# Attention with hardware loops over batches and head groups instead of unrolled code

## The reference

```python
q = (x @ Wq).reshape(b, s, 32, 32);  k, v = split(x @ Wkv)
scores = einsum('bqhd,bkd->bhqk', q, k) * 32**-0.5 + slope[h] * (kpos - qpos)   # causal
out = einsum('bhqk,bkd->bqhd', softmax(scores), v).reshape(b, s, h) @ Wo
x = layernorm(x + out)
rank = (8, 16, 32, 64)[argmax(x @ gate_w.T + gate_b)]
x = layernorm(x + x @ W.T + bias + (x @ A[:rank].T) @ B[:, :rank].T)
```

## Time and profile before

| | |
|---|---|
| time, median of 3 runs | 4088.18 us (4086.85 to 4093.12) |
| the profiled execution | 4086.85 us, span of its instructions 4085.0 us |
| PE busy | 3766.8 us, 92% of the span |
| DVE, ACT, POOL busy | 2474.2, 1925.0 and 1360.6 us |
| attention | up to about 3187 us of the span |
| feed-forward tiles | from about 3250 us to the end, 25.9 us each |

### The profile page before, as it was taken

One profiled execution on the slowest core, in us unless ns is written; L12 is line 12 of the kernel. 1 busy time (PEld: TensorE's weight loads), 2 busy tenths in 40 slices (PEclk: granted clock), 3 DMA queues, 4 the chain that ended last, 5 costly groups with the idle time before them and its releaser, 6 DMA issues. The chain is left out here.

```text
span 4085.0 us, 56649 instructions
## 1 busy us (share of the span) xinstructions
PE 3766.8 (92%) x22065; PEld 2354.1 (58%) x22065; DVE 2474.2 (61%) x4462; ACT 1925.0 (47%) x3253; POOL 1360.6 (33%) x420
## 2 busy tenths in 40 slices
PE   5989989999999997888999999999998599999998
PEld 3555555555454543555555554544443488888887
DVE  4557767776767672555776777676764344444444
ACT  2435655665666664344665666566666211111110
POOL 1113434444445453112433444455555100000000
PEclk8879999999999998888999999999999799999999
DMA  2111110000000001211111000000000412111111
GB/s 71 40 53 32 32 42 22 22 22 22 14 19 14 19 6 34 60 37 45 32 30 45 19 22 22 14 22 13 20 14 3 145 62 62 61 57 57 57 60 52
DMA packets 158918, 150.73 MB, mean 37 GB/s; under 512 B 8388, under 2 KB 141508, under 8 KB 156584
## 3 DMA queue, kind: packets, MB, share of 16 engines
q1 hardware_dynamic: 158696, 147.70, 12.4%
HBM read 96.75 MB, written 33.62 MB: 32 GB/s over the span
## 5 line engine op out<-in xcount | busy, mean ns | idle before, releaser
L494 ACT ACTIVATE prob<-ps_s,alibi 128x512 f32<-128x512 f32 (+3 forms) x2560 | 1521.6, 623 | 1110.5 <-PE ps_s L756 545.6
L574 DVE TENSOR_REDUCE mxp<-ps_a 128x1 f32<-128x512 f32 (+3 forms) x2560 | 1457.8, 605 | 800.7 <-PE ps_a L695 418.4
L437 POOL TENSOR_TENSOR prob<-prob 128x2048 f32<-128x2048 f32 (+1 forms) x240 | 1044.4, 4351 | 1126.5 <-ACT prob L494 1126.5
L756 PE MATMUL ps_s<-qst,kexp 97*128 97x512 f32 (+3 forms) x2560 | 1092.3, 437 | 74.5 <-ACT prob L494 55.1
L692 PE MATMUL ps_a<-kmax,qst 97*128 97x512 f32 (+3 forms) x2560 | 956.1, 399 | 34.3 <-DVE mxp L574 17.3
L756 PEld LDWEIGHTS ps_s<-qst,kexp 97*128 97x128 f32 x2560 | 492.3, 194 | 727.6 <-ACT prob L494 425.1
L779 PE MATMUL ps_o<-prob,val 128*32 128x512 f32 (+3 forms) x5120 | 612.2, 551 | 7.7 <-ACT prob L494 7.7
L692 PEld LDWEIGHTS ps_a<-kmax,qst 97*128 97x128 f32 x2560 | 504.3, 198 | 116.7 <-DVE mxp L574 59.5
L779 PE MATMUL ps_sum<-prob,ones 128*32 128x512 f32 (+3 forms) x3200 | 361.4, 525 | 0.0
L965 POOL TENSOR_TENSOR hb_sb<-h_sb,bias_b 128x1024 f32<-128x1024 f32 x32 | 76.8, 2401 | 791.9 <-DVE z_sb L1109 732.2
L592 DVE RECIPROCAL r_sb<-s_sb 128x128 f32<-128x128 f32 x256 | 233.4, 928 | 113.8 <-ACT s_sb L500 113.1
(11 more groups left out here) (148 smaller groups left out, 3709.3 us busy)
## 6 DMA issues: line engine op xcount, KB each, us to landing
wq_raw<-in_L_attn_Wq SPq DMA_DIRECT2D x65, 512.0 KB, 4.0
xs<-in_L_attn_hidden_states SPq DMA_DIRECT2D x9, 2048.0 KB, 8.7
qst<-qst SPq DMA_DIRECT2D x64, 256.0 KB
att_scratch<-at_sb SPq DMA_DIRECT2D x64, 256.0 KB, 2.4
at_raw<-att_scratch SPq DMA_DIRECT2D x32, 512.0 KB, 5.3
x_sb<-in_L_attn_hidden_states SPq DMA_DIRECT2D x32, 512.0 KB, 4.3
out<-z_sb SPq DMA_DIRECT2D x32, 512.0 KB, 3.2
z_sb<-in_L_attn_Wo SPq DMA_DIRECT2D x4, 512.0 KB, 5.1
```

The source lines that it names most:

```text
L437: nc.gpsimd.tensor_tensor(even[:, :, c1:], even[:, :, c1:], odd[:, :, c1:], ALU.add).then_inc(pair_done, 1)
L494: nc.scalar.activation(prob[slot][:, h, c0:], ps_s[bank][:, c0:], ACT.Exp, bias=alibi_of(u, h, k - QT * s)).then_inc(e_done, 1)
L574: nc.vector.tensor_reduce(mxp[:, h * QT + t, c:c + 1], ps_a[bank][:, 0:cols], AX.X, ALU.max).then_inc(a_done, 1)
L756: last = nc.tensor.matmul(ps_s[bank][:, c0:], kexp[0:KR, k * P:(k + 1) * P], qst[buf][0:KR, h, c0:], start=True, stop=not diagonal)
```

## The change

The loop over b becomes a hardware loop of 2 iterations. For s = 1, 2 and 3 the units 0 to 5 become a hardware loop of 2 iterations with 3 units in its body; units 6 and 7, and all units of s = 0, stay written out inside the loop over b. Buffers are picked by a number modulo 3, so three units in the body leave the buffers right. The order of the engine instructions stays the same. `counts` now moves its three totals into registers at the start of each unit.

```diff
-            for b in range(B):
+            with eng.Fori(0, B) as b:
                 prologue(b)
                 for s in range(NSEG):
                     more = s + 1 < NSEG
-                    for u in range(HG - 2):
-                        unit_step(b, s, u, u, plan_step(s, True, s, True, False, s > 0 or u > 0))
+                    if s == 0:
+                        for u in range(HG - 2):
+                            unit_step(b, s, u, u, plan_step(s, True, s, True, False, u > 0))
+                    else:
+                        with eng.Fori(0, 2) as i:
+                            for j in range(3):
+                                unit_step(b, s, i * 3 + j, j, plan_step(s, True, s, True, False, True))
                     unit_step(b, s, HG - 2, HG - 2, plan_step(s, True, s, more, more, True))
                     unit_step(b, s, HG - 1, HG - 1, plan_step(s, more, s + 1, more, False, True))
                 epilogue(b)
...
-        def counts(b, s, u):
-            return unit_no(b, s, u), START + b * TILES_B + tiles_before(s, u), START + b * STEPS_B + steps_before(s, u)
+        taken = []
+
+        def counts(eng, b, s, u):
+            taken.append(eng)
+            values = (unit_no(b, s, u), START + b * TILES_B + tiles_before(s, u),
+                      START + b * STEPS_B + steps_before(s, u))
+            regs = [eng.alloc_register(f"{name}_{len(taken)}") for name in ("unit", "tiles", "steps")]
+            for reg, value in zip(regs, values):
+                eng.reg_mov(reg, value)
+            return tuple(eng.snap(reg, min_val=low) for reg, low in zip(regs, (0, START, START)))
```

More of the change, by code:

```diff
@@ L424, in step @@
             def step(b, s, u, const, plan):
-                g, tiles, steps = counts(b, s, u)
+                g, tiles, steps = counts(pool, b, s, u)
                 for what, arg in plan:
@@ L476, in step @@
             def step(b, s, u, const, plan):
-                g, tiles, steps = counts(b, s, u)
+                g, tiles, steps = counts(act, b, s, u)
                 for what, arg in plan:
@@ L605, in step @@
             def step(b, s, u, const, plan):
-                g, tiles, steps = counts(b, s, u)
+                g, tiles, steps = counts(dve, b, s, u)
                 i = 0
@@ L719, in step @@
             def step(b, s, u, const, plan):
-                g, tiles, steps = counts(b, s, u)
+                g, tiles, steps = counts(pe, b, s, u)
                 buf = parity(s, const)
```

## The result

The changed kernel takes 4186.7 us in the median of 4 runs (4184.06 to 4193.92), the kernel before 4087.5 beside it: 1.0243 times as long, with a 95% interval of 1.0225 to 1.0261. That is 99 us more. The forecast was 4151 us, within 4118 to 4195. Direction and main mechanism held; the sum of 64 us was too small by a third.

The account below looks back on a forecast made before the run. The prediction took PE as the bound, held up by the latency loop between its scores and ACT's exponentials. Terms of 50 + 4 + 10 = 64 us on the profiled 4086.85 us gave 4151 us, range 4118 to 4195.

Parts of the forecast that it names:

- What bounds the kernel: Attention's score-exponential loop: PE bounds the unit, but latency exceeds its work, 1.28 us against 0.94 for two slots.
- Exponentials in the looped units: ACT, looped units: two register operations behind the score wait add 0.18 us on 276 turns, 50 us (41 to 61).
- Exponentials elsewhere: ACT in s = 0 and units 6 and 7: the register operation runs before the wait, so nothing is added.
- PE's register operations: Ahead of nearly each score matmul on PE: cost nothing, since PE's sequencer runs ahead of its array.
- PE's lead is lost at each wait: Rival, PE's score matmuls: register operations show twice each turn, 61 us more, 4212 us; chance 0.09.
- DVE's shift, and SP: End of looped units: one operation behind DVE's `c_max` wait, 4 us; `c_ps` and SP operations 0, at most 4.
- Loop edges: Six inner edges and one over b: taken branches wait for code, 1.4 us each, 10 us (2 to 25).
- edges cost much more: Rival, loop edges: engines' code misses add up to 76 us in place of 10, 4217 us; chance 0.06.
- Which edges miss: ACT's loop edges: s = 2, 3 and the outer miss, s = 1 may not, making the term 9 us for 10.
- Faster: Rival, PE's score loads: idle time without releaser is code fetching, loops save 73 us, giving 4078 us; chance 0.04.
- the dearer rivals: PE's lead lost at each wait (4212 us, chance 0.09) and edges costing much more (4217 us, chance 0.06).

Follow-up runs that it names:

- the copied bias: Changed kernel, with POOL copying the next unit's 64 bias columns to a fixed buffer so that ACT's bias address is constant: 4131.6 us, ratio 1.0087.
- the pauses kernel: Kernel before the change, with PE waiting for a POOL memset ahead of six units of s = 3, no branch added: one run, 4116.6 us.

## Why the prediction was right, and where its sum was short

*What bounds the kernel.* Held. The loop of latencies between score and exponential passed on the added 0.19 us in full: the turn was forecast at 1.46 us and is 1.47.

*Exponentials in the looped units.* Forecast 50 us, and right in size and cause. Taking the operations out of the looped kernel gives back 50 us by the units (48 with the copied bias), and adding them without a loop costs 48. I had 4, 7.5 and 11.5 turns for the three s; the growth by 0.59, 1.36 and 2.33 us with ACT alone looped, at 0.19 each, is 3.1, 7.1 and 12.1. The errors nearly cancel, 22.3 for my 23. The duration, taken from DVE's row, was right for ACT.

*Exponentials elsewhere, and PE's register operations.* Forecast nothing, and nothing is seen: gap 0.04 us in units 6 and 7, PE's steady units unchanged with PE alone looped. The rival "PE's lead is lost at each wait" falls with that.

*DVE's shift, and SP.* Forecast 4 us, at most 4 more. The steady units keep 8 us when ACT's operations are out, and 10.6 with DVE, POOL and SP looped alone, of which 4 go when DVE is written out. So DVE's 4 us fit; the row of waits that I priced them from doesn't show them, since PE's wait for the shift is 63.9 us in the changed kernel, for 65.9 before. What POOL and SP add, 7 us when looped without the others, I had bounded at 4.

*Loop edges.* This is the mis-sized term: 10 us forecast, 30 measured at the six inner edges and some 3 at the outer one, beyond my upper end of 25. I took 1.4 us an edge from the smallest landing, "a little of it covered by PE's lead". With PE alone looped an edge that misses costs 6.4 us: a stall of about 3.4 and then 3.0 for the half clock behind it; in the changed kernel the six cost 2.5 to 6.4, 4.9 on average. The upper end of 3.6 us for the stall would have been near (PE's branches take 3.5 to 3.6); the clock was in no part of my sum. The gap on ACT, forecast at 1 to 2 us, is 2.5 to 3.1 from its branch to the next operation. I had rows for a stall and asked only how long PE stands still, not what it runs at afterwards. Nor does PE's lead cover anything at an inner edge, since its own branch stalls. The rival "edges cost much more" named the wrong mechanism: the misses of engines do not add up (27 and 27 us alone, 30 together).

*Which edges miss.* By the rule of the Trainium skill ("Runtime: NRT & Kernel Launch", "Instruction fetch mechanics") I let the edge of s = 1 pass on ACT, whose body of 450 instructions is shorter than the 512 named there. (The loop of s = 1 has an edge in each b, so that the term would have been 7 us and not 9.) It missed: unit 3 of s = 1 took 39.57 us at 0.96. At 269 instructions, with the copied bias, it did not. The same section has the code come in blocks of 256 instructions and the window hold two of them, so a body of 450 can reach into a third; I had compared only its length. That the place counts is seen on DVE in the feed-forward loop, whose body of 266 instructions the change doesn't touch: its next operation stands 0.33 to 0.37 us behind the branch in the kernel before, and 2.95 to 3.00 in the changed one (at no cost, as the tiles are still 25.89 us apart). On PE, counting a weight load and its matmul as two, the body of s = 1 has 1592 instructions and was at hand, and that of s = 2 has 2183 and missed, where the page names 2048; for PE the trace agrees.

*Faster.* Idle time of score loads with no releaser fell from 261.3 to 241.0 us, though PE's four stalls of 4 us are in it now. What the rest of it is no run shows. No kernel came out below before.

*The rest.* Beyond the terms, 13 to 14 us of the 104 lie in s = 0 and in the last unit of each b. Nothing that loops there accounts for them, they come with more time at the low clock, and the written-out kernel with pauses has the longer last unit too. The time fell inside the range, 8 us under its upper end. That is in part luck: I had kept that width for the dearer rivals, which are both wrong, and it took in the clock, which I had not thought of.

## What to carry to other kernels

Where two engines wait for each other in turn, put nothing between a wait and the operation that it releases: two address operations there cost about 50 us of 4088, and a copy to a constant place, on an engine with time to spare, took them back. Count a taken branch whose body isn't at hand as a stall and as the slow clock after it, and count engines that miss at the same edge once, not one for each. A body's length alone doesn't say whether it is at hand. With few passes a prefetch for the branch taken is paid back at the exit.

## What the hardware showed that was not expected

PE's clock fell after pauses that look harmless: at 1.10 us of idle ahead of a unit it stayed, at 1.74 us it was 0.66 on average over the next 5 us, at 3.02 us 0.50. Each length was tried once. The length alone doesn't decide: in the last unit of the first b PE waits 1.21 us for ACT in the kernel before, and the clock stays; in the pauses kernel it waits 1.11 us there, and 13.7 us at the low clock follow.

The same seems to make kernels vary from run to run. A unit of s = 0 of the kernel before, and the same unit where DVE, POOL and SP loop:

```profile
130.30:157.48 27.18, 24.93 (x157) 0.81 0.16 40
```

```profile
129.31:153.30 23.99, 20.84 (x157) 1.00 0.18 45
```

PE's work is the same 157 matmuls on record, the clock isn't, and it is worth 3.2 us a unit. Over the traces the two passes of s = 0 took between 467 and 491 us, with no order by what was looped. The kernel before itself spread from 4073 to 4105 us over these groups.

What tips the clock there is open. PE's longest wait in such a unit is that for the shift, between the pause of 1.10 us that left the clock alone and the one of 1.74 that didn't. But it is as long in the unit that ran at full clock, so its length is not what tells the two apart. In the kernel before, and where DVE, POOL and SP loop:

```profile
PE ps_m L700 <- DVE shift L581: 1.2, 1, 1.2
```

```profile
PE ps_m L726 <- DVE shift L607: 1.2, 1, 1.2
```
